# Keys, values and the shared expert moved into the ends of the expert stage of a two-layer gated model

## The reference

```python
x = x + tanh(g_xattn[0]) * xattn0(layernorm(x), ctx)            # 16 heads of 16
x = x + tanh(g_ffn[0])   * moe(layernorm(x))                    # 64 experts, 8 per token, plus a shared expert
x = x + tanh(g_xattn[1]) * xattn1(layernorm(x), ctx, mask)      # keys and values are projections of ctx alone
x = x + tanh(g_ffn[1])   * ffn_int8(layernorm(x))               # fake-quantised, with two global maxima
# moe: at most 256 rows per expert, in order of arrival;
out = sum over a token's experts of weight * (silu(x w1) * (x w3)) w2
shared = (silu(x @ shared_gate.T) * (x @ shared_up.T)) @ shared_down.T
```

## Time and profile before

| what | value |
|---|---|
| median of 3 runs | 1888.5 us (1887.87 to 1895.99) |
| the profiled execution | 1888.42 us |
| its span | 1886.6 us |
| busy: PE, DVE, ACT, POOL | 1718.2, 1384.9, 1179.9, 613.1 us |
| HBM traffic | 129 GB/s over the span |

### The profile page before, as it was taken

The page is one execution under the profiler, slowest core; times in us unless marked ns, Lnnn a source line. Parts: engine busy times, 40 slices in busy tenths (PEclk is TensorE's granted clock), DMA queues, the critical chain, the costliest instruction groups (busy, mean ns, idle before and its releaser), DMA issues.

```text
span 1886.6 us, 54365 instructions
## 1 busy us (share of the span) xinstructions
PE 1718.2 (91%) x20198; PEld 1346.9 (71%) x20208; DVE 1384.9 (73%) x4589; ACT 1179.9 (63%) x2411; POOL 613.1 (32%) x617
## 2 busy tenths in 40 slices
PE   5999999999999499999999995899999999968855
PEld 3888888888887388888888884577777777743334
DVE  4788888888888446655544442688888888859988
ACT  3777777777777133333333331688888888858875
POOL 1000000000000147767667664322222222211147
PEclk9999999999999699999999998899999999989989
DMA  3222333222334568888888875323322322203265
GB/s 102 81 93 93 98 97 108 95 93 93 96 99 136 160 173 213 221 216 206 215 211 213 212 190 103 108 86 89 97 86 89 97 87 87 68 35 159 101 260 187
DMA packets 231349, 247.64 MB, mean 131 GB/s; under 512 B 29680, under 2 KB 207216, under 8 KB 228912
## 3 DMA queue, kind: packets, MB, share of 16 engines
q1 hardware_dynamic: 206272, 205.54, 34.0%
q0 software_dynamic: 24816, 38.62, 11.0%
HBM read 142.40 MB, written 101.66 MB: 129 GB/s over the span
## 4 chain that ended last, share of the span: by engine, by line
PE 62%; DVE 25%; ACT 8%; issue 2%; SPq 2%; DMA 1%; POOL 0%; POOLq 0%; DVEq 0%; ACTq 0%
DVE mt L806 15%; PE tiles L384 8%; PE tiles L367 7%; PE bank L1339 6%; ACT pt L585 6%; PE bank L449 6%; PE tiles L1314 6%; PE bank L1282 6%; PE bank L412 3%; PE tiles L351 3%; PE bank L1349 3%; PE bank L1326 3%; PE bank L479 3%; DVE hmax L1760 3%; DVE h_ring L1753 2%
## 5 line engine op out<-in xcount | busy, mean ns | idle before, releaser
L806 DVE TENSOR_REDUCE mt<-tiles 128x16 f32<-128x2048 f32 x128 | 293.5, 2293 | 56.6 <-PE tiles L367 56.6
L2016 POOL TENSOR_TENSOR rstd<-var,minus_half 128x2 f32<-128x2 f32 x140 | 97.7, 698 | 722.2 <-DVE var L885 703.5
L585 ACT ACTIVATE pt<-tiles 128x2048 f32<-128x2048 f32 x128 | 240.8, 1881 | 48.3 <-PE tiles L384 48.3
L1545 POOL DMA_INDIRECT accumulator<-ye,tid x128 | 210.0, 1641 | 118.3 <-DVE ye L1478 95.6
L1478 DVE TENSOR_SCALAR ye<-bank,xr 128x256 f32<-128x256 f32 x128 | 56.1, 480 | 180.7 <-PE bank L1326 180.7
L1530 POOL DMA_INDIRECT xr<-token_rows,tid x128 | 136.9, 1070 | 78.2 <-issue 37.9
L384 PE MATMUL tiles<-qm,qkp 32*128 32x128 f32 x4096 | 150.2, 283 | 6.7 <-DVE mt L806 2.7
L449 PE MATMUL bank<-xt,w_q 128*128 128x128 f32 x1024 | 154.5, 285 | 0.9 <-ACT xt L593 0.9
L367 PE MATMUL tiles<-qkp 32*128 32x256 f32 x2048 | 150.7, 407 | 3.3 <-ACT qkp L607 3.0
L384 PEld LDWEIGHTS tiles<-qm,qkp 32*128 32x128 f32 x4096 | 125.9, 186 | 36.3 <-DVE mt L806 21.6
L449 PEld LDWEIGHTS bank<-xt,w_q 128*128 128x128 f32 x1024 | 131.2, 194 | 14.9 <-issue 13.2
(11 more groups left out here) (247 smaller groups left out, 4141.4 us busy)
## 6 DMA issues: line engine op xcount, KB each, us to landing
keys_values<-res SPq DMA_DIRECT2D x64, 256.0 KB, 3.2
cxax<-accumulator SPq DMA_DIRECT2D x128, 128.0 KB, 2.3
cxax<-keys_values SPq DMA_DIRECT2D x128, 128.0 KB, 2.5
hidden_away<-h_ring SPq DMA_DIRECT2D x8, 1536.0 KB, 5.1
token_rows<-pay SPq DMA_DIRECT2D x64, 160.0 KB, 1.8
pt<-in_expert_up SPq DMA_DIRECT2D x36, 256.0 KB, 2.9
cxax<-in_ctx SPq DMA_DIRECT2D x64, 128.0 KB, 2.2
res<-in_x SPq DMA_DIRECT2D x64, 128.0 KB, 2.3
```

The costliest lines, as they stand in the source:

```text
L585: nc.scalar.activation(pt[r % 2][:, :, :], tiles[:, :, :], ACT.Exp).then_inc(sem("exp_done"), 1)
L806: nc.vector.tensor_reduce(mt[:, :].rearrange("p (i n c) -> p i n c", i=RT, n=2 * KC)[:, :, :, 0], tiles[:, :, :].rearrange("p i (n k) -> p ...
L1545: nc.gpsimd.indirect_dma_start(out=acc[p][:, :], out_offset=bass.IndirectOffsetOnAxis(ap=tid[b % 8][:, h:h + 1], axis=0), in_=ye[r][:, h, ...
```

## The change

It moves K/V and shared pieces out of the expert slots, into the end of layer 0's attention, into slots -3 to -1 and into new slots behind the last expert, E + 1 to E + 5 (65 to 69). The count of pieces is the same.

- K/V pieces 0 to 3 run in the last slots of layer 0's attention, in the score banks 0 to 3; 4 to 6 in slots -3 to -1; 52 in slots 0 to 63; 5 behind. Shared ups 0 and 1 and down 0 run after the last slot of layer 0's attention, in banks 7 and 4; ups 2 to 4 in slots -3 to -1; 54 in slots 0 to 63; 5 behind.
- SP: the K/V weights are loaded at slot 64 of layer 0's attention, the first shared inputs at slot 68, the weights of experts 1 to 6 at slot 66, all before the meeting; the eight mask loads go to expert slots 2 and 4. The last `store_row` goes one slot later. Four buffers for the K/V stores in place of two.
- The third meeting has three engines, PE, ACT and DVE; POOL and SP pass it. In place of it SP waits for all adds in slot 69 and loads the sums of blocks 0 and 1 there, and the first keys and values in slot 65. Later loads wait for the stores that they need.

```diff
-        kvs = [room(52 + 2 * k, 2) for k in range(2)]
+        kvs = [room(k, 2) for k in (52, 54, 4, 6)]
+        PHASES = {1: 5, 2: 10, 3: 13, 4: 18, 5: 23}
-            eng.wait_ge(sem("phase_done"), 5 * n)
+            eng.wait_ge(sem("phase_done"), PHASES[n])
-            for s in range(-MAP_AHEAD, E + 2):
+            for s in range(-MAP_AHEAD, E + 8):
+        KV_EARLY, SHARED_EARLY = 4, 2
+        PAIR_AT = numbered([-7, -6, -5, -4, -3, -2, -1] + [s for s in range(E) if s not in (5, 9, 14, 21, 27, 33, 39, 45, 51, 57, 60, 62)]
+                           + [E + 1, E + 2, E + 3, E + 4, E + 5])
+        SHARED_AT = numbered([-5, -4, -3, -2, -1] + [s for s in range(E) if s not in (8, 20, 23, 30, 36, 42, 48, 54, 56, 58)]
+                             + [E + 1, E + 2, E + 3, E + 4, E + 5])
+        def kv_bank(n):
+            return bank[n % 4] if n < KV_EARLY else bank[5]
+        def shared_bank(n):
+            return bank[4] if n < SHARED_EARLY and n % 2 else bank[7]
...
                     moe_counts(u)
+                    if v is not None and v[0] == NB - 2:
+                        keys_or_values(pe, (1, 1))
+                    if v is not None and v[0] == NB - 1:
+                        keys_or_values(pe, (2, 2))
+                        keys_or_values(pe, (3, 3))
...
                     output(o)
+                    if o is not None and o[0] == NB - 1:
+                        keys_or_values(pe, (0, 0))
...
+        FIRST_SUMS, SUMS_AT = 2, E + 5
+        def first_sums(sp):
+            sp.wait_ge(sem("e_up_done"), E)
+            for p in range(2):
+                sp.wait_ge(sem(f"e_added{p}"), 16 * E)
+            for b in range(FIRST_SUMS):
+                load_sums(sp, (b, b))
...
+                    if stage(1) is not None and stage(1)[0] == NB - 1:
+                        sp.wait_ge(sem("qk_done"), NB)
+                        sp.wait_ge(sem("v_done"), NB)
+                        keys_values_weights(sp)
+                    if stage(5) is not None and stage(5)[0] == NB - 1:
+                        for n in range(SHARED_IN):
+                            load_shared(sp, (n, n))
...
-                    if stage(5) is not None and stage(5)[0] == NB - 1:
+                    if stage(5) is not None and stage(5)[0] == NB - 3:
                         sp.wait_ge(sem("pv_done"), NB)
-                        first_expert_weights(sp, EARLY_FREE, 4)
-                    store_row(stage(5))
+                        sp.wait_ge(sem("at_done"), NB)
+                        first_expert_weights(sp, EARLY_FREE, WEIGHT_BUFFERS)
...
             if L == 0:
+                for n in range(KV_EARLY - 1):
+                    keep_pair(sp, (n, n))
                 load_steps((NB - 1, (NB - 1) % 4))
...
             def body(s, stage):
+                if s == E + 1:
+                    for b in range(FIRST_SUMS):
+                        load_keys_values(sp, (b, b))
+                if s == SUMS_AT:
+                    first_sums(sp)
...
+                if stage(0) is not None and stage(0)[0] in MASKS_IN_AT:
+                    masks_in(sp, MASKS_IN_AT[stage(0)[0]])
...
-            first_expert_weights(sp, 4, WEIGHT_BUFFERS)
-            masks_in(sp)
             expert_slots(body)
-            for p in range(2):
-                sp.wait_ge(sem(f"kv_kept{p}"), 8 * E)
-                sp.wait_ge(sem(f"sh_kept{p}"), 8 * NB)
...
             sp.wait_ge(sem("ffn_int_out"), 16 * 3)
-            phase_end(sp, 3)
...
             experts_pool(pool)
-            phase_end(pool, 3)
...
             attention_act(act, 0)
+            copy_pair(act, (3, 3))
+            for n in range(SHARED_EARLY):
+                shared_tanh(act, (n, n))
+            shared_out(act, (0, 0))
...
             attention_pe(pe, 0)
+            for n in range(SHARED_EARLY):
+                shared_up(pe, (n, n))
+            shared_down(pe, (0, 0))
```

More of the change, by code:

```diff
@@ L333, in attention_slots, with expert_slots, numbered @@
             slots(body, NB, first, NB + LAGS)
+        MAP_AHEAD, GATHER_AHEAD = 3, 2
+        def expert_slots(body):
+            for s in range(-MAP_AHEAD, E + 8):
+                body(s, lambda lag, s=s: (s - lag, (s - lag) % 4) if 0 <= s - lag < E else None)
+        def numbered(places):
+            return {s: (k, k % 4) for k, s in enumerate(places)}
+        KV_EARLY, SHARED_EARLY = 4, 2
[3 more added lines that the diff above has]
+                             + [E + 1, E + 2, E + 3, E + 4, E + 5])
+        assert len(PAIR_AT) == E and len(SHARED_AT) == NB
         FIRST = (-3, -3)
@@ L570, in attention_pe, with copy_pair, shared_tanh, shared_out @@
             attention_slots(body, FIRST[L])
+        def copy_pair(act, e):
+            if e is None:
+                return
+            n, r = e
+            p = r % 2
+            act.wait_ge(sem("kv_done"), n + 1)
+            wait(act, f"kv_kept{p}", 8 * (n - p) - 16)
+            nc.scalar.copy(kvs[n % 4], kv_bank(n)[:, :]).then_inc(sem("kv_out"), 1)
+        def shared_tanh(act, e):
+            if e is None:
+                return
+            n = e[0]
+            act.wait_ge(sem("sh_up_done"), n + 1)
+            wait(act, "sh_silu_done", n)
+            nc.scalar.activation(sth, shared_bank(n)[:, 0:FS], ACT.Tanh, scale=0.5).then_inc(sem("sh_th_out"), 1)
+        def shared_out(act, e):
+            if e is None:
+                return
+            n = e[0]
+            act.wait_ge(sem("sh_down_done"), n + 1)
+            if n < 2:
+                act.wait_ge(sem(f"x3_kept{n}"), 8 * NB)
+            wait(act, f"sh_kept{n % 2}", 8 * (n - n % 2))
+            nc.scalar.activation(ys[n % 2], shared_bank(n)[:, 0:D], ACT.Copy, scale=tg_half[:, 0:1]).then_inc(sem("sh_out"), 1)
         def attention_act(act, L):
@@ L710, in body @@
                         router_tanh(v)
+                    if v is not None and v[0] == NB - 1:
+                        copy_pair(act, (1, 1))
                     copy_counts(u)
+                    if v is not None and v[0] == NB - 1:
+                        copy_pair(act, (2, 2))
                     copy_v(f)
@@ L719, in body @@
                     copy_x2t(w)
+                    if w is not None and w[0] == NB - 1:
+                        copy_pair(act, (0, 0))
                     exponent(k)
@@ new lines, in keep_shared, with load_keys_values @@
+        def keep_shared(sp, e):
+            if e is None:
+                return
+            n = e[0]
+            sp.wait_ge(sem("sh_out"), n + 1)
+            sp.dma_start(shared[bass.ds(n * P, P), :], ys[n % 2]).then_inc(sem(f"sh_kept{n % 2}"), 16)
+        def load_keys_values(sp, n):
+            if n is None:
+                return
+            b, r = n
+            p = r % 2
+            wait(sp, "qk_out_1", 2 * (b - 1))
+            wait(sp, "v_out_1", b - 1)
+            for k in range(2):
+                sp.wait_ge(sem(f"kv_kept{k}"), 8 * (b - p) + 16)
+            sp.dma_start(kvt[p][:, 0:D].rearrange("p (c t) -> p c t", c=KC),
+                         keys_values[b - p].rearrange("p (c e t) -> p c e t", c=KC, e=2)[:, :, p, :]).then_inc(sem(f"kv_in{p}"), 16)
+            sp.dma_start(kvt[p][:, D:2 * D], keys_values[b - p + 1][:, p * D:(p + 1) * D]).then_inc(sem(f"kv_in{p}"), 16)
@@ new lines, in load_sums @@
+        def load_sums(sp, n):
+            if n is None:
+                return
+            b, r = n
+            p = r % 2
+            wait(sp, "sum_done_1", b - 1)
+            sp.wait_ge(sem(f"sh_kept{p}"), 8 * (b - p) + 16)
+            for n_ in range(2):
+                sp.dma_start(ax[p][:, n_, :], acc[n_][bass.ds(b * P, P), :]).then_inc(sem(f"ax_in{p}"), 16)
+            sp.dma_start(row(b), shared[bass.ds(b * P, P), :]).then_inc(sem(f"ax_in{p}"), 16)
+        FIRST_SUMS, SUMS_AT = 2, E + 5
@@ L1265, in slot_steps @@
                 last.then_inc(sem("e_steps_done"), 1)
[L1267 to L1283, removed]
             weights = weights_pe(pe)
@@ L1554, in experts_pool @@
             expert_slots(body)
-            for p in range(2):
-                pool.wait_ge(sem(f"e_added{p}"), 16 * E)
         assert IC == 6 and TPC == 4
@@ L2118, in _ @@
             attention_dve(dve, 0)
+            for n in range(SHARED_EARLY):
+                shared_silu(dve, (n, n))
             phase_end(dve, 2)
```

223 lines of the change are left out of this document (103 added, 120 removed).

## The result

The changed kernel takes 1863.3 us in the median (1860.5 to 1867.9, 4 runs), beside 1890.7 for the one before: a ratio of 0.9855, 95% interval 0.9834 to 0.9875, or 27 us. The forecast was 1856.5 us, in a range of 1848 to 1868. The profiled execution took 1860.5 us (span 1858.8), 27.9 less than the profiled one before.

What follows compares the result with a forecast made beforehand. The tensor engine bounds the expert stretch (busy 433.69 of 435 us), with idle PE in the joins on both sides. -39.5 + 9.3 - 2.5 = -32.7 from 1888.4 gives 1855.7; plus 0.8, 1856.5 us, range 1848 to 1868.

Steps and rivals of the forecast that it cites:

- Expert slots: First to last expert's up: 10 K/V and 8 shared pieces fewer, PE still setting the pace, 39.5 us less.
- 0.8 for issue gaps: Added to the summed time for issue gaps where a slot lost its cover: 0.8 us.
- Second join, new work: Behind the last expert: leftover slots of 5.32 us each; engines meet 32.7 us after the last up starts.
- Second join, the lead-in: DVE's first sum to layer 1's first maximum stays 10.1 us; maximum at U + 43.0 (U: last up's start), 9.3 longer.
- First join: End of layer 0 to expert slot 0: slot 0 at 661.0, 2.5 us earlier; bounds 4.5 earlier, 6 later.
- first rival: First join gives the time back: SP's longer queue and PE's half clock, meeting 4 to 6 us later; 1864.5 us, chance 0.12.
- sign of error: Prediction is wrong if the meeting at the end of layer 0 lies beyond 646 us.
- End of layer 1: No cost booked here; GpSimd's 4.63 us drain was taken to go out of the path at the second join.
- co-bound: Expert slots: GpSimd or DMA queues begin to hold PE, half of the 22.2 us shared gain lost; 1867 us, chance 0.08.
- the transfers set the slot: Expert slots: transfers are the limit, so removing PE work shortens nothing; slower, 1895 us, chance 0.04.
- better: Both joins: clock stays full and slot 0 starts at 659; 1852.7 us, chance 0.08.

## Why the prediction was right, and where it was off

The sign, the mechanism and the range held, and 27.4 us came of the 34.2 that the forecast means against the same runs (1890.7 less 1856.5). In the profiles it was 27.9 of 31.9, since the profiled run before took 1888.4. By its steps:

- *Expert slots*: -38.2 for -39.5. A piece is worth what the earlier trace rows gave, and PE still sets the pace. Of the missing 1.3, 0.6 is a wait of PE for gathered rows that the kernel before did not have, and 0.5 is the price of a shared piece: in the changed kernel a slot without a shared up takes 5.98 (from 924.96) and the next, without the down, 6.91, beside 7.80 for a full one, so the pair is worth 1.82 + 0.89 = 2.71 and not 2.77. A slot without a K/V piece takes 6.07, as forecast. The 0.8 for issue gaps covers part of this.
- *Second join, new work*: steps of 5.27 us for the 5.32 of the earlier trace rows. Sound.
- *Second join, the lead-in*: it starts 0.5 us after the last piece and takes 9.5 from DVE's first sum to the maximum, for 10.1. PE was idle for 4.20 us ahead of its first transposes (about 5 forecast). The query projection behind them still took 2.07, as before, at a granted clock of 0.50; the clock rose while the score matmuls ran (0.75 from 1156.8 to 1158.4), and they took 1.48 for 2.06. So 0.6 came back, between the 0 that I took and the 1.8 that I bounded. The forecast also has a slip: its terms give 29.5 + 1.4 + 0.86 + 0.5, so the last piece ends at U + 32.3, and it wrote 32.7; measured were 32.5.
- *First join*: this is the term that was mis-sized, -1.1 for -2.5. The part behind the meeting was right in this profile (17.9 for 17.6) and is 19.6 in the profiles with the half clock behind the meeting, a case that the forecast took into its bounds. The meeting came 2.6 us later than before, inside the stated 0 to 3, where the 661.0 for slot 0 means 1.5. PE was done when the forecast said (643 forecast; 644.3, of which 1.5 lie ahead of layer 0's last maximum). SP was not: its last table load was to land at 642.5 and landed at 645.9, or 644.4 without that 1.5. The queue is longer, the last issues wait for PE's input and the table's round trip, and three stores with two context loads stand ahead of the load from 640.64 to 643.18. The third of them needs the first one's landing, 2.14 us after its issue, which I had not seen. The load itself also takes longer (below). This is part of the first rival's mechanism. The first join came 1.4 us dearer than forecast, where the rival's price was 8. The forecast's own sign of error, a meeting beyond 646, was met by a hair (646.03), but only with the 1.5 us from ahead of the join. Over the seven profiles of this join slot 0 begins 59.8 to 62.3 us behind layer 0's last maximum, for 59.2 forecast and 61.7 in the one profile before; so the forecast was too low in all of them, and whether the first join itself got shorter at all isn't shown.
- *End of layer 1*: forecast 0, and it was +2.2, of which 1.12 is GpSimd's drain. I had booked the 4.63 us of the earlier trace rows as gone from the path. It was postponed to the next meeting that GpSimd takes part in. This is the step of the reasoning that failed: "all of the 4.63 drain and the load go out of the path". The other 1.1 stays open; the three kernels with an early drain still take 0.8 to 1.5 us more here than the kernel before.
- The 1.5 at the start can't be told from the scatter between profiles.

The rivals "co-bound" and "the transfers set the slot" fall: at a DMA share of 0.88 and a slot of 6.9 us, in the kernel with seven pieces behind, PE waited 0.4 us for gathered rows. The "better" case fell with the first join. The median of 1863.3 lies nearer to the first rival's 1864.5 than to the forecast, but not by that rival's doing: of the 4.1 us between forecast and measured profile, 1.4 are from the first join, 2.2 from the end of layer 1, 1.5 from the start, 0.5 from the slots (with the 0.8 for gaps), and 0.8 and 0.7 came back in the second join and layer 1. Some of these errors cancel, which is luck. The last table load, in the chain of waits before and then after:

```profile
639.83 1.93 DMA table<-table_rows
```

```profile
643.28 2.62 DMA table<-table_rows
```

Behind the stores and context loads it takes 0.7 us longer. This agrees with the rule of the Trainium skill that the forecast cited there (DMA: Bandwidth & Descriptors, on issuing engines).

## What to carry over

Work with no due time belongs into the stalls at both ends of a full stage, and its price there is read from the chain under it. Pieces behind the last expert cost little until they are as long as that chain (28.7 us here; three pieces cost 2.6 us), and more than in the stage after that, because neighbours no longer cover their waits. An engine that is taken out of a meeting takes its drain along to the next one. A wait that is moved behind another issue may end last there, so a value that a rival gave is checked against the chain before the rival is believed. And a meeting that comes earlier only for SP leaves PE idle ahead of it: where PE had idled 2.3 us or more there, the part behind the meeting took 19.8 us or more instead of 18.2.

## What the runs showed of the hardware that I had not expected

GpSimd's first drain after its indirect transfers took 4.63 us right behind them and 5.37 when it came over 500 us after the last of them, in nine profiles; where an earlier drain stood behind the adds, the one at that later place took 0.7. Profiles of nearly the same layer 0 differ by up to 7 us at its end. And one and the same first join ran at either level of PE's clock behind its meeting, which is worth 1.6 us.
